# Four heads of value products side by side in a 12-layer kernel on one core

## The reference, cut to what matters

```python
HEADS = 16                                  # head size 8
# L2 (causal)
sim = jnp.where(causal_mask, mask_value, einsum('bhid,bhjd->bhij', q, k))
e = jnp.exp(sim - max(sim))
num = jnp.einsum('bhij,bhjd->bhid', e, v)
den = jnp.sum(e, axis=-1, keepdims=True) + eps
out = (num / den).transpose(0, 2, 1, 3).reshape(B, N, D) @ Wo.T
# L3 (full)
attn = softmax(einsum('bqhd,bkhd->bhqk', q, k))
z = einsum('bhqk,bkhd->bqhd', attn, v).reshape(b, s, d)
out = z @ Wo.T + bo
```

## Time and profile before

| | |
|---|---|
| median of 3 runs | 3665.79 us |
| the profiled execution | 3671.47 us, its span 3669.7 us |
| PE busy | 2717.3 us, 74% of the span |
| DVE / ACT / POOL busy | 2483.2 / 1952.5 / 1690.0 us |
| granted TensorE clock, mean | 0.776 of full speed |

### The profile page before, as it was taken

How to read it: one execution, slowest core, us unless ns; L and a number is a source line. 1 busy time by engine, 2 the same in 40 slices (tenths; PEclk the granted TensorE clock), 3 DMA queues, 4 the chain that set the end, 5 groups by cost and what they waited for, 6 DMA issues and landing times.

```text
span 3669.7 us, 31626 instructions
## 1 busy us (share of the span) xinstructions
PE 2717.3 (74%) x8594; PEld 889.0 (24%) x8594; DVE 2483.2 (68%) x3598; ACT 1952.5 (53%) x3111; POOL 1690.0 (46%) x1349
## 2 busy tenths in 40 slices
PE   5314656788878888878578877879578867887887
PEld 1101212233222322222122322223122312232212
DVE  1688888878777787577976877677866774243351
ACT  3545645764847464755548465765367442732423
POOL 0587674465534572455635473446545451121101
PEclk6656656887878887878779786888578767978768
DMA  1122231222212230223212231223112220121100
GB/s 74 68 80 70 68 108 53 69 86 81 78 47 84 77 119 26 70 77 97 74 53 80 74 114 36 78 70 111 60 59 94 83 67 24 50 63 37 41 30 32
DMA packets 158880, 253.22 MB, mean 69 GB/s; under 512 B 18928, under 2 KB 56688, under 8 KB 158448
## 3 DMA queue, kind: packets, MB, share of 16 engines
q1 hardware_dynamic: 158704, 251.18, 21.2%
HBM read 233.81 MB, written 16.52 MB: 68 GB/s over the span
## 4 chain that ended last, share of the span: by engine, by line
PE 40%; DVE 22%; issue 12%; ACT 12%; DMA 6%; POOL 5%; SPq 2%; DVEq 0%; POOLq 0%; ACTq 0%
PE ps L458 40%; DVE rh L1152 6%; DMA cr<-shares 4%; DVE nmx L1075 4%; ACT L1189 3%; ACT ps L1444 2%; DVE xib L1131 2%; ACT tN L1391 1%; DVE xif L1131 1%; POOL rb L1500 1%; POOL tF L1514 1%; DMA Qs<-cTN 1%; SPq L1599 1%; POOL rh L1489 1%; DVE rh L1158 1%
## 5 line engine op out<-in xcount | busy, mean ns | idle before, releaser
L1152 DVE TENSOR_TENSOR_SCAN rh<-ps,rb 128x512 f32<-128x512 f32 x512 | 622.6, 1216 | 187.0 <-ACT ps L1444 172.6
L1075 DVE TENSOR_REDUCE nmx<-ps 128x1 f32<-128x512 f32 (+3 forms) x1024 | 549.6, 581 | 191.7 <-PE ps L458 189.9
L1391 ACT ACTIVATE tN<-ps 128x512 f32<-128x512 f32 (+3 forms) x1024 | 474.9, 516 | 235.9 <-PE ps L458 232.8
L1489 POOL TENSOR_TENSOR rh<-rh,cs 128x512 f32<-128x512 f32 x256 | 395.9, 1551 | 439.6 <-DVE rh L1152 439.4
L458 PE MATMUL ps<-tN,strip 128*64 128x512 f32 (+3 forms) x2048 | 507.3, 572 | 4.5 <-ACT tN L1391 4.2
L458 PE MATMUL ps<-hF,W 128*128 128x512 f32 x592 | 398.7, 761 | 83.8 <-DVE tF L1020 55.0
L1500 POOL TENSOR_TENSOR rb<-duf,bs 128x512 f32<-128x512 f32 x256 | 390.1, 1542 | 143.1 <-DVE rh L1152 129.5
L1189 ACT ACT_TABLE_LOAD x348 | 446.5, 1283 | 6.3
L1500 POOL TENSOR_TENSOR rb<-dub,bs 128x512 f32<-128x512 f32 x256 | 387.0, 1531 | 96.6 <-DVE rh L1152 96.3
L458 PE MATMUL ps<-tF,W 128*128 128x512 f32 x544 | 344.0, 729 | 95.3 <-POOL tF L1514 82.9
L1514 POOL TENSOR_TENSOR tF<-tF,cr 128x512 f32<-128x512 f32 x128 | 171.3, 1338 | 506.7 <-DMA cr<-shares 417.7
(11 more groups left out here) (228 smaller groups left out, 3627.1 us busy)
## 6 DMA issues: line engine op xcount, KB each, us to landing
cr<-shares SPq DMA_DIRECT2D x256, 256.0 KB
bs<-rowsf SPq DMA_DIRECT2D x128, 256.0 KB, 3.6
cs<-rowsf SPq DMA_DIRECT2D x128, 256.0 KB, 3.3
bs<-rowsb SPq DMA_DIRECT2D x128, 256.0 KB, 3.6
cs<-rowsb SPq DMA_DIRECT2D x128, 256.0 KB, 3.3
parts<-spl SPq DMA_DIRECT2D x32, 384.0 KB, 2.5
Qs<-parts SPq DMA_DIRECT2D x384, 32.0 KB
Ks<-parts SPq DMA_DIRECT2D x384, 32.0 KB
```

Of the source, the lines that this page charges most:

```text
L1075: red(nmx[:, qt, 8 * a + i:8 * a + i + 1], PA[u % 3][:, 0:nk], AX.X, ALU.max, negate=True).then_inc(s_red, 1)
L1152: eng.tensor_tensor_scan(rh[n % NH][:, g, :], PS, rb[n % NBB][:, g, :], 0.0, ALU.mult, ALU.add).then_inc(s_h, 1)
L1391: act(tN[e % NP][:, q0:T], PA[a][:, 0:T - q0], ACT.Exp).then_inc(s_ex, 1)
L1489: tt(h, h, cs[n % NB][:, :], ALU.mult).then_inc(s_cp, 1)
```

## The change

`values` now writes 32 columns for each of four heads: a quad of units (two p, two a) with the same key block goes to rows 0, 32, 64 and 96 of `O`, and only the first of the four waits, for the exponentials of all four. The stationary cut is 32 columns out of a strip of 48: zeros, values at 16 to 24, ones at 24 to 32, and the two cuts (m = 0, 1) put them on rows 16m and 16m + 8 of a block. There are eight strips instead of four, five `tN` tiles instead of four, and units are ordered so that the four of a quad follow each other. At the end of a group ACT copies `O` to `hN[g]` (`oc`), a product with the constant `den` spreads each sum over its 16 rows back in `O` (`sums`), ACT does one Ln and one Exp on 128 rows, and DVE one product. For group 0 this stands between the units of group 1: the copy after unit 33, the spreading product after the scores of units 34 and 35, Ln and Exp after unit 35. `hN[1]` shares memory with `tN[0]`. The output weights are spread to the new rows, 128 by 256, and the output product is two, one for each group. All order texts are new.

```diff
-        hN, rN = sb("hN", [128, T]), sb("rN", [128, T])
-        NP = 4
+        rN, NP = sb("rN", [128, T]), 5
         tN = [sb(f"tN{i}", [128, T]) for i in range(NP)]
+        hN = [sb("hN", [128, T]), tN[0]]
-        strips = [sb(f"strip{i}", [128, NT, 88]) for i in range(4)]
+        strips = [sb(f"strip{i}", [128, NT, 48]) for i in range(8)]
...
-        UNITS = [(g, p, t, a) for g in range(2) for p in range(4) for t in range(NT) for a in range(2)]
+        UNITS = [(g, 2 * m + p, t, a) for g in range(2) for m in range(2) for t in range(NT) for p in range(2) for a in range(2)]
...
                 def values(e):
                     g, p, kt, a = UNITS[e]
-                    q0 = 0 if l3 else 128 * kt
-                    eng.wait_ge(s_strip, 16 * n + 8 * g + 2 * p + a + 1)
-                    eng.wait_ge(s_ex, units + e + 1)
+                    q0, c = 0 if l3 else 128 * kt, 2 * (p % 2) + a
+                    if c == 0:
+                        eng.wait_ge(s_strip, 16 * n + 8 * g + 4 * (p // 2) + 4)
+                        eng.wait_ge(s_ex, units + e + 4)
                     if e == 32:
-                        eng.wait_ge(*j.dve("on0"))
-                    mm(O[64 * a:64 * a + 64, q0:T], strips[2 * (p % 2) + a][:, kt, 24 - 8 * p:88 - 8 * p], tN[e % NP][:, q0:T],
+                        eng.wait_ge(*j.act("ld0"))
+                    at = 16 - 16 * (p // 2)
+                    mm(O[32 * c:32 * c + 32, q0:T], strips[4 * (p // 2) + c][:, kt, at:at + 32], tN[e % NP][:, q0:T],
...
+                def sums(g):
+                    eng.wait_ge(*j.act(f"oc{g}"))
+                    mm(O, w("den"), hN[g][:, :]).then_inc(*A.by_pe(j, f"d{g}"))
...
-                for e in range(0, 64, 2):
+                for e in range(0, 64, 4):
                     scores(e)
                     scores(e + 1)
                     mask(e)
                     mask(e + 1)
                     yield
-                    if e >= 2:
-                        values(e - 2)
-                        values(e - 1)
-                        yield
-                values(62)
-                values(63)
-                yield
-                eng.wait_ge(*j.dve("on1"))
+                    if e:
+                        four(e - 4)
+                        yield
+                    scores(e + 2)
+                    scores(e + 3)
+                    mask(e + 2)
+                    mask(e + 3)
+                    yield
+                    if e == 32:
+                        sums(0)
+                        yield
+                four(60)
+                yield
+                sums(1)
+                yield
...
-                mm(R0, w(name + "o"), hN[:, :]).then_inc(*A.by_pe(j, "o"))
+                for g in range(2):
+                    eng.wait_ge(*j.dve(f"on{g}"))
+                    last = mm(R0, w(name + "o", 128 * g, 128 * g + 128), hN[g][:, :], start=g == 0, stop=g == 1)
+                last.then_inc(*A.by_pe(j, "o"))
...
-                    tt(hN[32 * g:32 * g + 32, :], O[0:32, :], rN[0:32, :], ALU.mult)
-                    tt(hN[64 + 32 * g:96 + 32 * g, :], O[64:96, :], rN[32:64, :], ALU.mult).then_inc(*A.by_dve(j, f"on{g}"))
+                    tt(hN[g][:, :], hN[g][:, :], rN[:, :], ALU.mult).then_inc(*A.by_dve(j, f"on{g}"))
...
+                def take(g):
+                    eng.wait_ge(s_pv, units + 32 * g + 32)
+                    act(hN[g][:, :], O, ACT.Copy).then_inc(*A.by_act(j, f"oc{g}"))
...
+                for e in range(64):
+                    weigh(e)
+                    yield
+                    if e == 33:
+                        take(0)
+                        yield
+                    if e == 35:
+                        yield from divide(0)
+                take(1)
+                yield
+                yield from divide(1)
...
-                            pair = 8 * n + 4 * g + p
-                            if pair >= 2:
-                                eng.wait_ge(s_pv, 8 * (pair - 1))
+                            four = 4 * n + 2 * g + p // 2
+                            if four >= 2:
+                                eng.wait_ge(s_pv, 16 * (four - 1))
...
+    c["den"] = (k[:, None] % 16 == 8) & (k[:, None] // 16 == k[None, :] // 16)
```

More of the change, by code:

```diff
@@ L1 @@
+import itertools
 from contextlib import ExitStack
@@ L65 @@
[L65 to L74, removed]
@@ L149 @@
+        "L1A4L1A2L1A2L1A1L1A1L2A2L1A2L1A2L1A48F4A2F1A68F5"
     ),
     "pool": (
[L151 to L154 removed]
@@ L1384, in attention, with weigh @@
                 R0, R1, O = PA
-                for e, (g, p, kt, a) in enumerate(UNITS):
+                def weigh(e):
+                    g, p, kt, a = UNITS[e]
                     q0 = 0 if l3 else 128 * kt
@@ L1391, in attention, with divide @@
                     act(tN[e % NP][:, q0:T], PA[a][:, 0:T - q0], ACT.Exp).then_inc(s_ex, 1)
-                    yield
-                    if e % 32 == 31:
-                        eps_ = {0: 0.0, 1: 0.0} if l3 else {0: eps[32:64, 1:2], 1: eps[96:128, 1:2]}
-                        use(LE)
-                        eng.wait_ge(s_pv, units + e + 1)
-                        act(rN[0:32, :], O[32:64, :], ACT.Ln, bias=eps_[0]).then_inc(*A.by_act(j, f"dl{g}"))
-                        act(rN[32:64, :], O[96:128, :], ACT.Ln, bias=eps_[1]).then_inc(*A.by_act(j, f"dr{g}"))
-                        yield
-                        use(LE)
-                        eng.wait_ge(*j.act(f"dr{g}"))
-                        act(rN[0:64, :], rN[0:64, :], ACT.Exp, scale=-1.0).then_inc(*A.by_act(j, f"rd{g}"))
-                        yield
+                def take(g):
+                    eng.wait_ge(s_pv, units + 32 * g + 32)
+                    act(hN[g][:, :], O, ACT.Copy).then_inc(*A.by_act(j, f"oc{g}"))
+                def divide(g):
+                    use(LE)
+                    eng.wait_ge(*j.pe(f"d{g}"))
+                    if g:
+                        eng.wait_ge(*j.dve("on0"))
+                    act(rN[:, :], O, ACT.Ln, bias=0.0 if l3 else e8).then_inc(*A.by_act(j, f"ld{g}"))
+                    yield
+                    use(LE)
+                    eng.wait_ge(*j.act(f"ld{g}"))
+                    act(rN[:, :], rN[:, :], ACT.Exp, scale=-1.0).then_inc(*A.by_act(j, f"rd{g}"))
+                    yield
[4 more added lines that the diff above has]
+                        take(0)
+                        yield
+                    if e == 35:
[3 more added lines that the diff above has]
+                yield from divide(1)
             def strand_l():
@@ L1542, in pool_engine @@
             for t in strips:
-                last = eng.memset(t[:, :, 56:64], 1.0)
+                last = eng.memset(t[:, :, 24:32], 1.0)
             last.then_inc(s_setg, 1)
@@ L1679, in layout, with spread @@
         c[p + "al"], c[p + "dd"], c[p + "op"] = halves(i[q + "A_log"]), halves(i[q + "D"]), halves(i[q + "out_proj"].T)
+    def spread(a):
+        out = np.zeros((128, 2, a.shape[1]), np.float32)
+        for g, p, h in itertools.product(range(2), range(4), range(2)):
+            head, at = 8 * h + 4 * g + p, 32 * (2 * (p % 2) + h) + 16 * (p // 2)
+            out[at:at + DH, g] = a[DH * head:DH * head + DH]
+        return out.reshape(128, -1)
     c["lng"], c["lnb"] = i["L1_attn_ln_g"][:, None], i["L1_attn_ln_b"][:, None]
@@ L1686, in layout @@
     c["a2q"], c["a2k"], c["a2v"] = i["L2_attn_Wq"].T, i["L2_attn_Wkv"][0:128].T, i["L2_attn_Wkv"][128:256].T
-    c["a2o"] = i["L2_attn_Wo"].T
+    c["a2o"] = spread(i["L2_attn_Wo"].T)
     for j, n in enumerate("qkv"):
```

205 lines of the change are left out of this document (110 added, 95 removed), and 4 rows, old and new, of the table GROUPS.

## The result

The changed kernel takes **3680.8 us** (median of 18 runs) against 3666.8 of the kernel before on the same chips: ratio 1.0035, 95% interval 1.0023 to 1.0047. It is slower by 0.35%, where 3578 us, 88 less than before, was forecast. Its profiled execution took 3684.36 us, with a mean granted clock of 0.729 (before 0.776).

What follows compares the result with a forecast made beforehand. No engine was full; PE came first with 40% of the chain. PE's net 199 us counted at 54% gave -107, bare groups +24, DVE -5: -88 us, to 3578 us, own range 3530 to 3620 (50%).

Steps and rivals of the forecast that it cites:

- the first rival: Value products: the array takes only two tiles at a time, a quad costs 2.02 us; 3691 us, chance 10%.
- The added full products: PE: 48 more full products, three per attention for spreading sums and output weights, at about 1.2 us: 55 us.
- 0 for the ends: Group ends: copy, spreading product and fewer Ln and DVE steps cancel over 16 attentions, -16 and +22 as ends.
- -5 for DVE: DVE gives up 32 products of 0.69 us, 22 us, counted at its 22% of the chain.
- What of it is on the path: PE's net saving of 199 us counted at 54%, the chain's share of PE's busy time: -107 us.
- Where it isn't given: About five bare groups of 32, with no other strand's work between, keep a 2.9 us round: +24 us back.
- The clock falls with it: Rival: in bare groups thinly used PE gets the half clock, round 3.9 us; 3648 us, chance 8%.
- The five tiles pace it: Rival: waiting for whole quads costs ACT what PE gains, L3 attentions give next to nothing; 3634 us, chance 15%.
- The orders: 0: New order texts everywhere move things by some 20 us either way, sign unreadable, counted as 0.
- PE's 2520 us: Sign of being right: PE busy near 2520 us in all, from 2717.3 before.
- the bare round of 2.9 us: Sign of being right: four units in bare groups take 2.9 us, ACT idle before a quad's second exponential.
- the mixed one near 3.7: Sign of being right: a four-unit round in mixed stretches near 3.7 us, from 4.77 less the quad's 1.01.

Runs made afterwards that it cites:

- early_six_tiles: Changed kernel with each quad issued between the two score products of its pair, and six `tN` tiles instead of five: 3734.6 us, ratio 1.0189 to the kernel before.

## Why the prediction was wrong

**What was right.** Four tiles run four at a time and cost what a pair costs (1.00 us at the full clock), so that the first rival was wrong. Of the two estimates for a quad, the trace's 1.01 us held, not the 1.27 that I had worked out from the Trainium skill, "TensorE: Matmul & The Clock Gate", section "Measured speedup vs the span model". (The 65 us of PE between the two would be 35 us at 54%, not 25.) The added full products cost 60 us of PE (55 forecast). Layout, added products and ends together cost +10 us (pairs under before's orders against before), where +30 for the products, 0 for the ends and -5 for DVE, +25, was forecast.

**The step that failed: what the quads give, in "What of it is on the path" and "Where it isn't given".** Without the added products the forecast for the quads alone was 254 x 0.54 less 24, -113 us. Measured by undoing just that, quads against pairs under the new orders, they cost **+102 us** (3578.4 to 3680.8), and +158 under the old ones. Three things are in it.

The first is the round. My sketch of it was right in kind at the full clock, but the 1.3 us up to the quad's end are a score product of 0.3 and a quad of 1.0 and nothing else; the wakeups on either side were left out. The exponential that was to run beside the quad runs beside the score product ahead of it, because that product too waits for the quad's last exponential (there are two score banks), and it ends 0.1 us into the quad. So the round is 3.18 us at the full clock, not 2.9, with ACT idle for 1.03, not 0.8. A sixth tile takes this 0.3 away again (2.87), and quads then cost 17 us and not 102 (3577.3 to 3594.6). The run early_six_tiles shows that a tile is worth nothing when the score product that should fill it stands behind the quad.

The second is the clock, which the sum held at what it was. It fell to 0.50 and 0.61 in the last two bare groups, and from 0.93 to 0.74 over the 32 stretches between the first exponential of a group and its last; with pairs of 32 it is 0.92 there. At the half clock the round is 4.50 us: of its 1.64 us over two pairs at the full clock, 0.3 is the round's and 1.3 the clock's.

The third is the reach. I gave the lost round to 5 groups of 32 and took PE's saving at 54% in the rest. But the 32 stretches are 107 us longer than with pairs (1192 to 1299 in sum), which is the whole loss, 0.4 us for each of 256 rounds. The share of the chain is the share of waits that PE ends now; it doesn't say that what PE saves is saved, when the engine that feeds it has to stop for the saving.

**The rivals.** "The clock falls with it" had the right sign and came nearest to what the bare rounds show, but said 3.9 us for a round that takes 4.50, in 40 rounds and some others, where most stretches lost clock. Its reason doesn't stand: in the row at 3513 PE's records cover 31.31 of 32 us, so that the row doesn't show a thinly used PE. "The five tiles pace it" named the buffer that mattered, with too small a price: it let the L3 attentions gain nothing, where they lose. How the 102 us divide between waits and clock in the mixed stretches no run separates, since what shortened the waits also raised the clock; nor does any run show why it falls with quads and stays up with pairs.

**"The orders: 0"** was the second large miss, -99 us, and hides the first in the result. I had 20 us either way, and read nothing in the order for it. Which engine's text brings it stays open; exchanging them one by one wasn't tried.

**The sum.** Forecast: -113 (quads) + 30 (added products) + 0 (ends) - 5 (DVE) + 0 (orders) = -88. Measured: +102 (quads), +10 (products, ends, DVE and layout), -99 (orders) = +13; the medians differ by 14. The split hangs on the order in which it is made, since quads and orders act on each other: taken the other way it is +10 + 158 - 155. That the total came out near nothing is chance, two large effects that cancel. PE's 2520 us failed as well: in the 2747.3 the scores that wait within their records and other products at the lower clock have taken the place of what the value products gave up. Of the signs named, the bare round of 2.9 us, the mixed one near 3.7 and PE's total did not come; a clock well under 0.9 in a bare group, named as a sign of being wrong, did. For the mixed one the trace has 4.68 us, from the quad at 3588.05 to that at 3592.73, with three full products between.

## What to carry to other kernels

When two engines feed each other through a few buffers, batching one side's work saves time only if the buffers hold a batch and what the other side needs next as well: count every buffer on the loop (here tiles and score banks), write out one round with all its waits and wakeups, at both clocks, and do so before taking any share of the chain. Where work is taken off PE, ask what the round costs if the granted clock falls: in a bare round here that was four times what the added wait cost. Change the grouping and the order of a program one at a time: here one cost 102 us and the other gained 99, and together they looked like next to nothing.

## What the runs showed of the hardware that I had not expected

Four 32-column f32 products of 512 columns into four quarters of one bank take 1.00 us at the full clock and 1.86 at the half one, as much as two of 64 columns (1.01 and 1.91). And the granted clock doesn't follow the busy share of PE's records: in the bare groups it was 0.50 with 29.68 of 33 us busy, and 1.00 with 11.79 of 19, in the window of group 1 of the last attention with six tiles and four banks:

```profile
3505.00:3524.00 19.00, 11.79 (x90) 2.21 (x82) 0.69 (x1) 14.60 (x29) 0.00 (x0) 1.00 0.00 1
```

The same products are in both. In the first (the window at 3479 of the changed kernel) PE stands still for about 0.2 us several times a round between single score products, in the second once for 1.05 us; whether that is the cause no run shows.
